# A relational graph layer on one core: weights loaded first, means read from the statistics tile, six of eight normalisations on GpSimd, every fourth mask on ScalarE, filler matmuls in the first PE gaps

## The chip, the cores and the metric

One core of a Trainium2 chip runs the whole kernel. The metric is the device time of one execution in microseconds (us), lower is better. PE is TensorE, DVE VectorE, ACT ScalarE, POOL GpSimd; SP is SyncE, which here only issues DMAs.

## The reference, cut to what matters

There are 128 graphs (B) of 128 nodes (N) with 128 features (D), all fp32, and an int32 adjacency per graph whose entries are 0 or 1. The reference knows 40 relations, but entries above 1 never occur in these inputs, so that only relation 1, the "loop" direction, gives something:

```
h   = relu((x - mean(x)) / sqrt(var(x) + 1e-5))       # per node
p   = h @ W_loop.T
g   = p @ Wg_loop.T
v   = (p + b_loop) * sigmoid(g + bg_loop)
agg = (adj == 1).T @ v                                # per graph
out = x + relu(agg)
```

A general path for the other relations stands behind a branch at the end of the kernel. It is taken only if a sum over the adjacency says that an entry is neither 0 nor 1, and isn't taken here.

## The kernel before, in words

The graphs are worked on in 32 groups of 4 (GROUP), and two groups make a chunk (CHUNK), which is what one load or store of 512 KB moves. All of x and adj has its own place in SBUF (x_all, adj_all), the output is written over x_all and stored from there. Each engine has a queue written out by hand, with semaphores between the queues; nothing is scheduled by a planner. For group g these steps are done:

- row_stats(g) on DVE (L500): two bn_stats, each on two graphs, give per node a count, a mean and a sum of squared deviations for each graph, into the tile stats.
- coefficients, once per chunk, on POOL (L304 to L312): var_eps, mean_neg (the mean times -1), rstd as var_eps to the power -0.5, and shift = mean_neg * rstd. coef_ready is given behind the last.
- normalise(g), one instruction per graph into xn: POOL (L324) and DVE (L519) compute (x + mean_neg) * rstd, ACT (L393) computes x * rstd + shift. shares(g) says who takes which of the four graphs: in an even group POOL 3 and DVE 1; in an odd group POOL 2, DVE 1, ACT 1; in the first two groups DVE 2 and ACT 2.
- turn_rows(g) on PE (L715): four transposes into PSUM. It waits for all engines that normalised.
- relu_turned(g) on ACT (L404) writes hT_hi, rounded to fp32r; low_part(g) on DVE (L545) writes the remainder hT_lo.
- seed(g) on ACT (L411) writes both biases into the PSUM tile that the products add to.
- products(g) on PE: per graph hi by w_hi (L728), hi by w_lo (L729), lo by w_hi (L733), 256 columns wide: p and g at once.
- sigmoid(g) on ACT (L426), messages(g) on DVE (L535).
- edges(g) on POOL (L335) converts the group's adjacency to fp32 into one of four mask slots (MASKS). watch(c) on ACT (L432) sums the adjacency of chunk c for the branch at the end.
- aggregate(g) on PE (L750), output(g) on DVE (L560), and a store on SP (L228).

The loops run over t. PE does turn_rows(t+2), products(t+1), aggregate(t). DVE does messages(t), normalise(t+3), output(t-1), low_part(t+2), row_stats(t+6). ACT does normalise(t+3), relu_turned(t+2), seed(t+2), sigmoid(t+1) and in even t watch. POOL does, in even t, the coefficients of the chunk that holds group t+4, then edges(t+1), then normalise(t+4). xn has four slots, so normalise(g) waits until group g-4 is turned.

Before the loop: ACT's queue issues the two bias rows and then the two 64 KB weight matrices (L375 to L378), SP's queue the loads of x and adj. PE runs four matmuls on zeros, spreads the biases over the partitions with one matmul (L699), turns the weights (L688, L689), multiplies them (L691), and turns group 0. ACT copies bias_all out of PSUM, seeds group 0, and only then copies the turned weights (L443, L444, L446). At the end SP issues three stores: groups 30, the first half of 31, and the second half.

Of the kernel before, what the change touches and what calls it, by code (L numbers as in the profile page):

```python
# [12 lines left out]
GROUP = 4  # L13
# [5 lines left out]
def build(nc, x, adj, W_fwd, W_bwd, W_loop, Wg_fwd, Wg_bwd, Wg_loop,  # L19
# [12 lines left out]
    XN = 4  # L32

    ctx = ExitStack()
    with ctx:
# [16 lines left out]
        stats = sb("stats", [128, 2, PAIRS, 6])  # L52
        mean_neg = sb("mean_neg", [128, 2, CG])
        var_eps = sb("var_eps", [128, 2, CG])
        rstd = sb("rstd", [128, 2, CG])
        shift = sb("shift", [128, 2, CG])
# [44 lines left out]
        first_pow = sem("first_pow")  # L101
# [3 lines left out]
        pow_ready = sem("pow_ready")  # L105
# [3 lines left out]
        normed_act = sem("normed_act")  # L109
# [6 lines left out]
        mask_ready = sem("mask_ready")  # L116
        summed = sem("summed")
# [81 lines left out]
        def shares(g):  # L199

            if g < 2:
                return range(0), range(0, 2), range(2, 4)
            if g % 2 == 0:
                return range(0, 3), range(3, 4), range(4, 4)
            return range(0, 2), range(2, 3), range(3, 4)

        def act_norms(g):

            return g + 1 if g < 2 else 2 + (g - 1) // 2
# [11 lines left out]
        def _(sp):  # L221
# [16 lines left out]
            load_tile(x_all, x, 0, 0, GROUP, x_first)  # L238
            load_tile(x_all, x, GROUP, GC, CG - GROUP, x_loaded[0])
# [18 lines left out]
            sp.wait_ge(half_out, 1)  # L258
            store_tile((GROUPS - 1) * GROUP, (GROUPS - 1) * GC, GROUP // 2)
# [33 lines left out]
        def _(pool):  # L293
# [7 lines left out]
            def coefficients(p, lo, hi, var_done, pow_done, at, done):  # L301

                st = stats[:, p, lo // 2:hi // 2, :].rearrange("p k (e f) -> p k e f", e=2)
                pool.tensor_scalar(var_eps[:, p, lo:hi].rearrange("p (k e) -> p k e", e=2), st[:, :, :, 2],  # L304
                                   1.0 / D, EPS, ALU.mult, ALU.add).then_inc(var_done, 1)
                pool.tensor_scalar(mean_neg[:, p, lo:hi].rearrange("p (k e) -> p k e", e=2), st[:, :, :, 1],
                                   -1.0, 0.0, ALU.mult, ALU.add)
                pool.wait_ge(var_done, at)
                pool.tensor_tensor(rstd[:, p, lo:hi], var_eps[:, p, lo:hi], minus_half[:, lo:hi], ALU.pow  # L309
                                   ).then_inc(pow_done, 1)  # L310
                pool.wait_ge(pow_done, at)
                pool.tensor_tensor(shift[:, p, lo:hi], mean_neg[:, p, lo:hi], rstd[:, p, lo:hi], ALU.mult  # L312
                                   ).then_inc(done, 1)

            def normalise(g):

                s, p = g % XN, g // CHUNK % 2
                if g % CHUNK == 0:
# [3 lines left out]
                for j in shares(g)[0]:  # L322
# [15 lines left out]
            def chunk_coefficients(c):  # L338

                pool.wait_ge(stats_ready, c + 1)  # L340
                if c >= 2:
                    pool.wait_ge(normed_dve, (c - 1) * CHUNK)
                    pool.wait_ge(normed_act, act_norms((c - 1) * CHUNK - 1))
                coefficients(c % 2, GROUP if c == 0 else 0, CG, var_ready, pow_ready, c + 1, coef_ready)

            pool.wait_ge(first_stats, 1)
            coefficients(0, 0, GROUP, first_var, first_pow, 1, first_coef)
            chunk_coefficients(0)
            chunk_coefficients(1)
# [23 lines left out]
        def _(act):  # L373
            act.preload_act_table(ACT.Sigmoid)  # L374
            act.dma_start(bias_row[0:1, 0, :], b_loop).then_inc(bias_loaded, 16)  # L375
            act.dma_start(bias_row[0:1, 1, :], bg_loop).then_inc(bias_loaded, 16)
# [3 lines left out]
            def normalise(g):  # L380

                s, p = g % XN, g // CHUNK % 2
                if not shares(g)[2]:
                    return
                if g == 0:
                    act.wait_ge(first_coef, 1)
                else:
                    act.wait_ge(coef_ready, g // CHUNK + 1)
                if g >= XN:
                    act.wait_ge(turned, g - XN + 1)  # L390
# [437 lines left out]
```

## Time and profile before

| | us |
|---|---|
| median of 3 runs | 113.37 (111.84 to 114.14) |
| profiled execution, its own time | 112.11 |
| its span in the profile | 110.3 |
| busy PE, DVE, ACT, POOL | 98.8, 94.0, 91.8, 87.1 |
| granted TensorE clock in every slice | 9 or more tenths |

The span runs from the first to the last instruction. In the rows further down "xn<-x_all" reads: writes xn, reads x_all; "x3" is a count; L numbers are lines of the kernel before. Instructions of one engine overlap a little, so the next often starts 0.05 to 0.1 us before the recorded end of the one ahead. What an instruction costs its queue is therefore the distance from its start to the next start.

### The profile page before, as it was taken

To read this page: it belongs to the slowest core of one execution; us is meant where nothing else is said; L and a number is where in the kernel's file an instruction comes from. 1 tells how busy PE (TensorE), PEld (TensorE's weight loads), DVE (VectorE), ACT (ScalarE), POOL (GpSimd) and SP (SyncE) were. 2 spreads that over 40 slices of the span, in tenths; PEclk is the share of its full clock that TensorE was granted. 3 is DMA by queue.
4 is the path that set the end of the run, shared out by engine and by line. 5 is a ranking of instruction groups with operands and counts; after the bars stand their busy time and mean duration, and the time that the engine had idled before them with its cause. 6 is when DMAs were issued, how large, how long until landed. Compare 5 with 4: busy or idle time off the path is not lost.

```text
span 110.3 us, 2526 instructions
## 1 busy us (share of the span) xinstructions
PE 98.8 (90%) x780; PEld 92.1 (83%) x780; DVE 94.0 (85%) x202; ACT 91.8 (83%) x153; POOL 87.1 (79%) x182
## 2 busy tenths in 40 slices
PE   5524789899999999999999999999999999999970
PEld 1113569789999999999999999999999999999960
DVE  1508529899999999999999999999999999897780
ACT  4137533999999999999999999999999999999650
POOL 2380790999999999999999999999999999995000
PEclk9999999999999999999999999999999999999999
DMA  2999999999999999999999999980606050515067
GB/s 73 281 311 281 286 290 291 292 291 292 291 317 311 343 332 321 320 320 321 305 320 301 260 309 274 317 222 6 190 6 190 6 180 10 158 38 176 14 185 207
DMA packets 50275, 25.48 MB, mean 231 GB/s; under 512 B 850, under 2 KB 50260, under 8 KB 50260
## 3 DMA queue, kind: packets, MB, share of 16 engines
q1 hardware_dynamic: 49968, 25.17, 81.6%
q10 hardware_dynamic: 292, 0.13, 0.5%
q8 instruction: 7, 0.11, 0.4%
q14 instruction: 8, 0.07, 0.2%
HBM read 16.91 MB, written 8.39 MB: 229 GB/s over the span
## 4 chain that ended last, share of the span: by engine, by line
PE 80%; DMA 5%; POOL 3%; DVE 3%; issue 2%; ACT 2%; ACTq 1%; DVEq 0%; POOLq 0%
PE psum L750 23%; PE psum L715 16%; PE psum L728 14%; PE psum L729 13%; PE psum L733 13%; DMA w_raw<-in_L_gnn_Wg_loop 5%; POOL rstd L309 1%; DVE x_all L560 1%; DVE stats L500 1%; POOL xn L324 1%; PE psum L691 1%; ACT xn L393 1%; ACT hT_hi L404 1%; ACT L374 1%; PE psum L688 0%
## 5 line engine op out<-in xcount | busy, mean ns | idle before, releaser
L728 PE MATMUL psum<-w_hi,hT_hi 128*128 128x256 f32 x128 | 35.1, 307 | 1.8 <-issue 0.8
L750 PE MATMUL psum<-vals,mask 128*128 128x128 f32 x256 | 33.6, 275 | 0.0
L411 ACT ACTIVATE psum<-bias_all 128x1024 f32<-128x1024 f32 x32 | 32.9, 1027 | 0.1
L324 POOL TENSOR_SCALAR xn<-x_all,mean_neg,rstd 128x128 f32<-128x128 f32 x75 | 32.8, 449 | 0.1
L729 PE MATMUL psum<-w_lo,hT_hi 128*128 128x256 f32 x128 | 32.4, 285 | 0.0
L750 PEld LDWEIGHTS psum<-vals,mask 128*128 128x128 f32 x256 | 31.2, 191 | 0.1
L728 PEld LDWEIGHTS psum<-w_hi,hT_hi 128*128 128x128 f32 x128 | 24.7, 193 | 2.8 <-issue 1.7
L309 POOL TENSOR_TENSOR rstd<-var_eps,minus_half 128x8 f32<-128x8 f32 (+1 forms) x17 | 26.6, 1564 | 0.0
L500 DVE BATCH_NORM_STATS2 stats<-x_all 128x6 f32<-128x256 f32 x64 | 23.9, 416 | 2.7 <-DMA x_all<-in_x 2.7
L535 DVE TENSOR_TENSOR vals<-psum,gate 128x512 f32<-128x512 f32 (+1 forms) x33 | 21.7, 659 | 4.3 <-ACT gate L426 4.2
L729 PEld LDWEIGHTS psum<-w_lo,hT_hi 128*128 128x128 f32 x128 | 24.8, 193 | 0.0
L404 ACT ACTIVATE hT_hi<-psum 128x512 fp32r<-128x512 f32 x32 | 19.0, 593 | 5.1 <-PE psum L715 5.1
L545 DVE SCALAR_TENSOR_TENSOR hT_lo<-psum,hT_hi 128x512 fp32r<-128x512 f32 x32 | 21.7, 678 | 1.8 <-ACT hT_hi L404 1.8
L715 PE MATMUL psum<-ident,xn 128*128 128x128 f32 x128 | 20.9, 288 | 1.4 <-ACT xn L393 1.2
L560 DVE SCALAR_TENSOR_TENSOR x_all<-psum,x_all 128x512 f32<-128x512 f32 (+1 forms) x33 | 21.7, 663 | 0.1
L426 ACT ACTIVATE gate<-psum 128x512 f32<-128x512 f32 (+1 forms) x33 | 19.0, 575 | 3.3 <-PE psum L733 3.3
L733 PE MATMUL psum<-w_hi,hT_lo 128*128 128x256 f32 x128 | 20.9, 284 | 0.0
L335 POOL CAST mask<-adj_all 128x512 f32<-128x512 int32 x32 | 19.4, 611 | 0.0
L715 PEld LDWEIGHTS psum<-ident,xn 128*128 128x128 f32 x128 | 14.9, 145 | 4.3 <-POOL xn L324 2.8
L432 ACT ACTIVATE junk<-adj_all,minus_half 128x1024 bf16<-128x1024 int32 x16 | 18.2, 1140 | 0.0
L733 PEld LDWEIGHTS psum<-w_hi,hT_lo 128*128 128x128 f32 x128 | 17.9, 193 | 0.0
L519 DVE TENSOR_SCALAR xn<-x_all,mean_neg,rstd 128x128 f32<-128x128 f32 x34 | 14.8, 439 | 0.3 <-POOL shift L312 0.3
(34 smaller groups left out, 34.2 us busy)
## 6 DMA issues: line engine op xcount, KB each, us to landing
adj_all<-in_adj SPq DMA_DIRECT2D x16, 512.0 KB, 6.6
x_all<-in_x SPq DMA_DIRECT2D x15, 512.0 KB, 6.7
out<-x_all SPq DMA_DIRECT2D x15, 512.0 KB, 4.4
x_all<-in_x SPq DMA_DIRECT2D x2, 256.0 KB, 3.1
out<-x_all SPq DMA_DIRECT2D x1, 256.0 KB, 2.5
out<-x_all SPq DMA_DIRECT2D x2, 128.0 KB, 2.5
w_raw<-in_L_gnn_W_loop ACTq DMA_DIRECT2D x1, 64.0 KB, 3.2
w_raw<-in_L_gnn_Wg_loop ACTq DMA_DIRECT2D x1, 64.0 KB, 5.3
```

What stands on the lines that cost most here:

```text
L309: pool.tensor_tensor(rstd[:, p, lo:hi], var_eps[:, p, lo:hi], minus_half[:, lo:hi], ALU.pow).then_inc(pow_done, 1)
L324: last = pool.tensor_scalar(xn[:, s, j * D:j * D + D], x_all[:, g * GC + j * D:g * GC + j * D + D], mean_neg[:, p, k:k + 1], rstd[:, p, k: ...
L411: nc.scalar.activation(prod_ps[s].rearrange("p g a d -> p g (a d)"), bias_all[:, :, :].rearrange("p a d -> p (a d)").unsqueeze(1) .to_broa ...
L500: last = nc.vector.bn_stats(stats[:, c % 2, (g % CHUNK * GROUP + j) // 2, :], x_all[:, g * GC + j * D:g * GC + (j + 2) * D].rearrange("p ( ...
L535: nc.vector.tensor_tensor(per_graph(vals[:, s, :])[:, some, :], prod_ps[s][:, some, 0, :], per_graph(gate[:, s, :])[:, some, :], ALU.mult) ...
L545: nc.vector.scalar_tensor_tensor(out=hT_lo[:, s, :], in0=hT_ps[s], scalar=0.0, in1=hT_hi[:, s, :].bitcast(FP32), op0=ALU.max, op1=ALU.subt ...
L560: nc.vector.scalar_tensor_tensor(out=cols, in0=sums_ps, scalar=0.0, in1=cols, op0=ALU.max, op1=ALU.add).then_inc(half_out if more else out ...
L715: last = nc.tensor.transpose(hT_ps[s][:, j * N:j * N + N], xn[:, g % XN, j * D:j * D + D], ident[:, :])
L728: nc.tensor.matmul(to, hi, w_hi[:, :], start=False, stop=False, skip_group_check=True)
L729: nc.tensor.matmul(to, hi, w_lo[:, :], start=False, stop=False, skip_group_check=True)
L733: last = nc.tensor.matmul(to, lo, w_hi[:, :], start=False, stop=True, skip_group_check=True)
L750: last = nc.tensor.matmul(to[:, j * D:j * D + D], mask[:, g % MASKS, j * N:j * N + N], vals[:, s, j * D:j * D + D], start=True, stop=True)
```

## The change

- The weights' DMAs become the first of ACT's queue; the bias rows' DMAs move to SP's queue, behind the first load of x.
- mean_neg, shift and the semaphores for them are gone. normalise reads the mean from the stats tile and subtracts it. stats gets four slots (STAT_SLOTS) instead of two.
- POOL normalises 3 graphs of every group (1 in each of the first two), DVE the rest, ACT none.
- The mask of every group with g % 4 == 3 is made by ACT with a Copy; POOL skips it.
- ACT copies the turned weights out ahead of its first seed. DVE normalises group 0 ahead of the weights' remainders.
- PE gets 15 matmuls on zeros, bf16, 256 columns, whose results nobody reads: 3, 3, 5 and 4, at four places before the loop.
- The first half of the last group is stored from ACT's queue, not SP's.

```diff
@@ SP @@
             load_tile(x_all, x, 0, 0, GROUP, x_first)
+            sp.dma_start(bias_row[0:1, 0, :], b_loop).then_inc(bias_loaded, 16)
+            sp.dma_start(bias_row[0:1, 1, :], bg_loop).then_inc(bias_loaded, 16)
             load_tile(x_all, x, GROUP, GC, CG - GROUP, x_loaded[0])
...
-            sp.wait_ge(half_out, 1)
-            store_tile((GROUPS - 1) * GROUP, (GROUPS - 1) * GC, GROUP // 2)
             sp.wait_ge(out_ready, GROUPS)
             store_tile(B - GROUP // 2, (B - GROUP // 2) * D, GROUP // 2)
@@ shares @@
+        def pool_share(g):
+            return 1 if g < 2 else 3
+        def mask_by_act(g):
+            return g % MASKS == MASKS - 1
+        def masks_before(g, by_act):
+            return sum(mask_by_act(k) == by_act for k in range(g))
+        def mean_of(g, j):
+            k = g % CHUNK * GROUP + j
+            return stats[:, g // CHUNK % STAT_SLOTS, k // 2, 1 + k % 2 * 3:2 + k % 2 * 3]
@@ POOL @@
-                pool.tensor_scalar(mean_neg[:, p, lo:hi].rearrange("p (k e) -> p k e", e=2), st[:, :, :, 1],
-                                   -1.0, 0.0, ALU.mult, ALU.add)
                 pool.wait_ge(var_done, at)
                 pool.tensor_tensor(rstd[:, p, lo:hi], var_eps[:, p, lo:hi], minus_half[:, lo:hi], ALU.pow
-                                   ).then_inc(pow_done, 1)
-                pool.wait_ge(pow_done, at)
-                pool.tensor_tensor(shift[:, p, lo:hi], mean_neg[:, p, lo:hi], rstd[:, p, lo:hi], ALU.mult
                                    ).then_inc(done, 1)
...
-                        mean_neg[:, p, k:k + 1], rstd[:, p, k:k + 1], ALU.add, ALU.mult)
+                        mean_of(g, j), rstd[:, p, k:k + 1], ALU.subtract, ALU.mult)
...
+            normalise(0)
             chunk_coefficients(0)
+            normalise(1)
             chunk_coefficients(1)
...
-                if live(t + 1):
+                if live(t + 1) and not mask_by_act(t + 1):
                     edges(t + 1)
@@ ACT @@
-            act.dma_start(bias_row[0:1, 0, :], b_loop).then_inc(bias_loaded, 16)
-            act.dma_start(bias_row[0:1, 1, :], bg_loop).then_inc(bias_loaded, 16)
...
+            def edges(g):
+                act.wait_ge(adj_loaded[g // CHUNK], 16)
+                if g >= MASKS:
+                    act.wait_ge(summed, g - (MASKS - 1))
+                nc.scalar.activation(mask[:, g % MASKS, :], adj_all[:, g * GC:g * GC + GC], ACT.Copy
+                                     ).then_inc(mask_act, 1)
...
             for t in range(GROUPS):
-                if live(t + 3):
-                    normalise(t + 3)
...
                 if t % CHUNK == 0:
                     watch(t // CHUNK)
+                if live(t + 2) and mask_by_act(t + 2):
+                    edges(t + 2)
+            act.wait_ge(half_out, 1)
+            act.dma_start(
+                out[B - GROUP:B - GROUP // 2, :, :].rearrange("b n d -> n b d"),
+                x_all[:, (B - GROUP) * D:(B - GROUP // 2) * D].rearrange("p (b d) -> p b d", b=GROUP // 2)
+            ).then_inc(stored, 16)
@@ DVE @@
-                if g % CHUNK == 0 and c >= 2:
-                    dve.wait_ge(coef_ready, c - 1)
+                if g % CHUNK == 0 and c >= STAT_SLOTS:
+                    dve.wait_ge(normed_pool, (c - STAT_SLOTS + 1) * CHUNK)
...
-                for j in shares(g)[1]:
+                for j in range(pool_share(g), GROUP):
...
+            normalise(0)
             split_weights(0)
-            normalise(0)
             split_weights(1)
@@ PE @@
+            def keep_busy(times, where):
+                for _ in range(times):
+                    nc.tensor.matmul(bank[where][:, 0:256], zeros[:, 0:128], zeros[:, 0:256], start=True, stop=True)
+            keep_busy(3, 1)
             pe.wait_ge(ones_ready, 1)
             pe.wait_ge(bias_loaded, 32)
...
             turn_weights(w_raw[:, 0, :], w_raw[:, 1, :], w_gT[:, :], w_turned, w_gT_ready, 1)
+            keep_busy(3, 1)
...
             turn_rows(0)
+            keep_busy(5, 1)
             pe.wait_ge(w_lo_ready, 2)
             products(0)
             turn_rows(1)
+            keep_busy(4, 6)
             products(1)
```

How the queues change, at three places. POOL's queue over the chunk that holds groups 4 and 5 and the next one's first rows, before (rstd is the power, xn a normalisation, mask an adjacency conversion):

```order
L304 TENSOR_SCALAR var_eps<-stats 128x8
L306 TENSOR_SCALAR mean_neg<-stats 128x8
L309 TENSOR_TENSOR rstd<-var_eps,minus_half 128x8
L312 TENSOR_TENSOR shift<-mean_neg,rstd 128x8
L335 CAST mask<-adj_all 128x512
L324 TENSOR_SCALAR xn<-x_all,mean_neg,rstd 128x128 x3
L335 CAST mask<-adj_all 128x512
L324 TENSOR_SCALAR xn<-x_all,mean_neg,rstd 128x128 x2
L304 TENSOR_SCALAR var_eps<-stats 128x8
```

POOL's queue over groups 4 to 7 now:

```order
L305 TENSOR_SCALAR var_eps<-stats 128x8
L308 TENSOR_TENSOR rstd<-var_eps,minus_half 128x8
L333 CAST mask<-adj_all 128x512
L322 TENSOR_SCALAR xn<-x_all,stats,rstd 128x128 x3
L333 CAST mask<-adj_all 128x512
L322 TENSOR_SCALAR xn<-x_all,stats,rstd 128x128 x3
L305 TENSOR_SCALAR var_eps<-stats 128x8
L308 TENSOR_TENSOR rstd<-var_eps,minus_half 128x8
L322 TENSOR_SCALAR xn<-x_all,stats,rstd 128x128 x3
L333 CAST mask<-adj_all 128x512
L322 TENSOR_SCALAR xn<-x_all,stats,rstd 128x128 x3
```

Two short instructions per chunk are gone, one normalisation per chunk has come, and in every second chunk the first of the two conversions is gone.

ACT's queue from its start to its first sigmoid, before:

```order
L375 DMA bias_row<-in_L_gnn_b_loop 1x128
L376 DMA bias_row<-in_L_gnn_bg_loop 1x128
L377 DMA w_raw<-in_L_gnn_W_loop 128x128
L378 DMA w_raw<-in_L_gnn_Wg_loop 128x128
L437 ACTIVATE bias_all<-psum 128x256
L411 ACTIVATE psum<-bias_all 128x1024
L443 ACTIVATE w_gT<-psum 128x128
L444 ACTIVATE w_hi<-psum 128x128
L446 ACTIVATE w_hi<-psum 128x128
L393 ACTIVATE xn<-x_all,shift,rstd 128x128 x2
L411 ACTIVATE psum<-bias_all 128x1024
L404 ACTIVATE hT_hi<-psum 128x512
```

The same stretch now:

```order
L374 DMA w_raw<-in_L_gnn_W_loop 128x128
L375 DMA w_raw<-in_L_gnn_Wg_loop 128x128
L424 ACTIVATE bias_all<-psum 128x256
L427 ACTIVATE w_gT<-psum 128x128
L428 ACTIVATE w_hi<-psum 128x128
L398 ACTIVATE psum<-bias_all 128x1024
L433 ACTIVATE w_hi<-psum 128x128
L398 ACTIVATE psum<-bias_all 128x1024
L391 ACTIVATE hT_hi<-psum 128x512
```

The weights come ahead of everything, the first seed (L398) stands behind the two weight copies, and no normalisation is left in the queue.

PE's queue from the weights to the first products of group 0, now (before, the same without the rows that read only zeros):

```order
L691 MATMUL psum<-zeros 128x256 x3
L696 MATMUL psum<-bias_row,ones 128x256
L678 MATMUL psum<-ident,w_raw 128x128
L679 MATMUL psum<-ident,w_raw 128x128
L681 MATMUL psum<-w_gT,w_raw 128x128
L691 MATMUL psum<-zeros 128x256 x3
L710 MATMUL psum<-ident,xn 128x128 x4
L691 MATMUL psum<-zeros 128x256 x5
L723 MATMUL psum<-w_hi,hT_hi 128x256
```

## Rows read from the trace of the kernel before

**Rows 1.** The chain that ended last: start us, us, what; the start.

```profile
1.97 5.34 DMA w_raw<-in_L_gnn_Wg_loop
7.45 0.45 PE psum L688
...
9.58 0.77 ACT xn L393 x2
...
13.13 0.21 PE psum L728
...
23.46 0.66 PE psum L715 x4
```

**Rows 2.** Who waited for whom: us in total, times, longest us.

```profile
PEld psum L715 <- POOL xn L324: 2.8, 14, 0.3
```

**Rows 3.** POOL in order of time, one turn of its loop: start us, us.

```profile
59.18 0.20 POOL L304 TENSOR_SCALAR var_eps<-stats 128x8 f32<-128x8 f32 x1
59.46 0.20 POOL L306 TENSOR_SCALAR mean_neg<-stats 128x8 f32<-128x8 f32 x1
59.62 1.64 POOL L309 TENSOR_TENSOR rstd<-var_eps,minus_half 128x8 f32<-128x8 f32 x1
61.34 0.20 POOL L312 TENSOR_TENSOR shift<-mean_neg,rstd 128x8 f32<-128x8 f32 x1
61.48 0.61 POOL L335 CAST mask<-adj_all 128x512 f32<-128x512 int32 x1
62.08 1.31 POOL L324 TENSOR_SCALAR xn<-x_all,mean_neg,rstd 128x128 f32<-128x128 f32 x3
...
63.93 0.88 POOL L324 TENSOR_SCALAR xn<-x_all,mean_neg,rstd 128x128 f32<-128x128 f32 x2
64.89 0.20 POOL L304 TENSOR_SCALAR var_eps<-stats 128x8 f32<-128x8 f32 x1
```

**Rows 4.** DVE in order of time, the same stretch.

```profile
61.57 0.60 DVE L519 TENSOR_SCALAR xn<-x_all,mean_neg,rstd 128x128 f32<-128x128 f32 x1
62.09 0.68 DVE L560 SCALAR_TENSOR_TENSOR x_all<-psum,x_all 128x512 f32<-128x512 f32 x1
62.70 0.67 DVE L545 SCALAR_TENSOR_TENSOR hT_lo<-psum,hT_hi 128x512 fp32r<-128x512 f32 x1
63.29 0.75 DVE L500 BATCH_NORM_STATS2 stats<-x_all 128x6 f32<-128x256 f32 x2
63.97 0.67 DVE L535 TENSOR_TENSOR vals<-psum,gate 128x512 f32<-128x512 f32 x1
64.56 0.33 DVE L519 TENSOR_SCALAR xn<-x_all,mean_neg,rstd 128x128 f32<-128x128 f32 x1
64.81 0.68 DVE L560 SCALAR_TENSOR_TENSOR x_all<-psum,x_all 128x512 f32<-128x512 f32 x1
```

**Rows 5.** The last normalisations of POOL and DVE, in order of time.

```profile
98.22 0.92 POOL L324 TENSOR_SCALAR xn<-x_all,mean_neg,rstd 128x128 f32<-128x128 f32 x2
98.48 0.34 DVE L519 TENSOR_SCALAR xn<-x_all,mean_neg,rstd 128x128 f32<-128x128 f32 x1
```

**Rows 6.** ACT's groups of the page: busy us, mean ns, idle before.

```profile
L411 ACT ACTIVATE psum<-bias_all 128x1024 f32<-128x1024 f32 x32 | 32.9, 1027 | 0.1
L404 ACT ACTIVATE hT_hi<-psum 128x512 fp32r<-128x512 f32 x32 | 19.0, 593 | 5.1 <-PE psum L715 5.1
L432 ACT ACTIVATE junk<-adj_all,minus_half 128x1024 bf16<-128x1024 int32 x16 | 18.2, 1140 | 0.0
```

**Rows 7.** A DMA issue of the page: queue, KB, us from issue to landing.

```profile
w_raw<-in_L_gnn_W_loop ACTq DMA_DIRECT2D x1, 64.0 KB, 3.2
```

**Rows 8.** POOL at the start, in order of time.

```profile
6.08 0.20 POOL L312 TENSOR_TENSOR shift<-mean_neg,rstd 128x4 f32<-128x4 f32 x1
```

**Rows 9.** The chain that ended last, of 100 us to the end.

```profile
101.14 0.12 PE psum L728
```

**Rows 10.** SP's queue in order of time, the last stores.

```profile
106.52 1.49 SPq L228 DMA_DIRECT2D out<-x_all  x3
```

More of the change, by code:

```diff
@@ L32, in build @@
     XN = 4
+    STAT_SLOTS = 4
     ctx = ExitStack()
@@ L51, in build @@
         mask = sb("mask", [128, MASKS, GROUP * N])
-        stats = sb("stats", [128, 2, PAIRS, 6])
-        mean_neg = sb("mean_neg", [128, 2, CG])
+        stats = sb("stats", [128, STAT_SLOTS, PAIRS, 6])
         var_eps = sb("var_eps", [128, 2, CG])
         rstd = sb("rstd", [128, 2, CG])
-        shift = sb("shift", [128, 2, CG])
         minus_half = sb("minus_half", [128, CG])
@@ L299, in _, with coefficients @@
             pool.wait_ge(half_ready, 1)
[L301 to L303 removed]
+            def coefficients(c, lo, hi, var_done, at, done):
+                p = c % 2
+                st = stats[:, c % STAT_SLOTS, lo // 2:hi // 2, :].rearrange("p k (e f) -> p k e f", e=2)
                 pool.tensor_scalar(var_eps[:, p, lo:hi].rearrange("p (k e) -> p k e", e=2), st[:, :, :, 2],
                                    1.0 / D, EPS, ALU.mult, ALU.add).then_inc(var_done, 1)
[L306 to L307 removed]
                 pool.wait_ge(var_done, at)
                 pool.tensor_tensor(rstd[:, p, lo:hi], var_eps[:, p, lo:hi], minus_half[:, lo:hi], ALU.pow
[L310 to L312 removed]
                                    ).then_inc(done, 1)
@@ L317, in normalise @@
                 s, p = g % XN, g // CHUNK % 2
-                if g % CHUNK == 0:
+                if g == 0:
+                    pool.wait_ge(first_coef, 1)
+                elif g % CHUNK == 0 or g == 1:
                     pool.wait_ge(coef_ready, g // CHUNK + 1)
@@ L321, in normalise @@
                     pool.wait_ge(turned, g - XN + 1)
-                for j in shares(g)[0]:
+                for j in range(pool_share(g)):
                     k = g % CHUNK * GROUP + j
@@ L374, in _ @@
             act.preload_act_table(ACT.Sigmoid)
-            act.dma_start(bias_row[0:1, 0, :], b_loop).then_inc(bias_loaded, 16)
-            act.dma_start(bias_row[0:1, 1, :], bg_loop).then_inc(bias_loaded, 16)
             act.dma_start(w_raw[:, 0, :], W_loop).then_inc(w_loaded, 16)
             act.dma_start(w_raw[:, 1, :], Wg_loop).then_inc(w_loaded, 16)
[L380 to L390, printed above, removed]
-                for j in shares(g)[2]:
-                    k = g % CHUNK * GROUP + j
-                    last = nc.scalar.activation(
-                        xn[:, s, j * D:j * D + D], x_all[:, g * GC + j * D:g * GC + j * D + D], ACT.Identity,
-                        bias=shift[:, p, k:k + 1], scale=rstd[:, p, k:k + 1])
-                last.then_inc(normed_act, 1)
+            def edges(g):
[4 more added lines that the diff above has]
+                                     ).then_inc(mask_act, 1)
             def relu_turned(g):
@@ L438, in _ @@
                                  ).then_inc(bias_ready, 1)
+            act.wait_ge(w_turned, 1)
+            nc.scalar.activation(w_gT[:, :], bank[6][:, 128:256], ACT.Copy).then_inc(w_gT_ready, 1)
+            nc.scalar.activation(w_hi[:, 0:D], bank[6][:, 0:D], ACT.Copy).then_inc(w_hi_ready, 1)
             act.wait_ge(bits_set, 1)
@@ L520, in normalise @@
                         xn[:, s, j * D:j * D + D], x_all[:, g * GC + j * D:g * GC + j * D + D],
-                        mean_neg[:, c % 2, k:k + 1], rstd[:, c % 2, k:k + 1], ALU.add, ALU.mult)
+                        mean_of(g, j), rstd[:, c % 2, k:k + 1], ALU.subtract, ALU.mult)
                 last.then_inc(normed_dve, 1)
```

31 lines of the change are left out of this document (6 added, 25 removed).

## The prediction, made before the changed kernel ran

> **What bounds the kernel now.** I read the chain that ended last first. It is PE almost from end to end, but it starts with a DMA: the second weight matrix is issued at 1.97, flies for 5.34, and PE turns the weights only from 7.45. The first transposes of group 4, from which on the loop runs evenly, start at 23.46 [rows 1]. So there are two things: a start of 23.5 us and a loop. For the loop I read who waits for whom. PE's weight loads for the transposes wait for a POOL normalisation 14 times, 2.8 us in total, 0.2 each and 0.3 at most [rows 2]: once per two groups, from group 4 to group 30. I then read POOL in order of time. From one var_eps to the next, 59.18 to 64.89, it has no gap: POOL works 5.71 us per two groups and sets the period [rows 3]. Without its wait PE would need 5.71 - 0.20 = 5.51. DVE, the same way, by the distance from one start to the next: an output 0.61, a low part 0.59, a statistics pair 0.68, vals 0.59, and a normalisation 0.25 at 64.56 but 0.52 at 61.57 [rows 4]. With both normalisations short that is 2 x (0.61 + 0.59 + 0.68 + 0.59 + 0.25) = 5.44; the 0.27 more makes 5.71. The long one ends (62.17) just behind POOL's mask conversion (62.09), so I read it as DVE held up by POOL. Three engines stand within 0.3 us of each other per two groups: POOL 5.71, PE 5.51, DVE 5.44 plus what POOL takes from it.
>
> **The loop, part by part.** POOL loses mean_neg (59.46 to 59.62, 0.16 us) and shift (61.34 to 61.48, 0.14, and some 0.08 of waiting for the power's semaphore ahead of it). It gains one normalisation: from 62.08 to 63.93 stand three of them and a conversion, which takes 0.60 (61.48 to 62.08), so one costs (63.93 - 62.08 - 0.60) / 3 = 0.42. It loses a conversion of 0.60 in every second chunk, 0.30 on average [rows 3]. The sum is 5.71 - 0.16 - 0.22 + 0.42 - 0.30 = 5.45; some of the 0.28 between var_eps and mean_neg stays as the wait ahead of the power. POOL falls under PE's 5.51, but only by 0.06. The order helps: the coefficients of a chunk can start as soon as DVE's statistics pair ends, where POOL was 0.8 us late before (59.18 against the end of a pair, 5.71 before 63.29 + 0.75, or 58.33). So POOL has that as a reserve, and PE's wait should go. That gives 2.8 - 0.33 (the first of the 14 belongs to the start) = 2.5 us. Bounds: 0, if another engine holds the period at 5.71, and 2.5. I take 2.5, because both other engines' own work lies under 5.51 in the rows.
>
> DVE normalises one graph per group as before and reads the mean from another tile, which costs nothing: the operand has the same shape. What can change is the hold-up. The mean of the two (0 and 0.27) is already 0.13 per normalisation. POOL now spends 6 x 0.42 of 5.5 us in normalisations and 0.9 in conversions. Does a POOL normalisation hold up DVE? The one place that shows it is at the end: two of POOL's run from 98.22 and take 0.92 instead of 0.88, and DVE's own, from 98.48 on in the middle of them, takes 0.34, hardly more than at 64.56 [rows 4, 5]. So DVE got through and POOL paid 0.04. If the hold-up of 0.27 falls away DVE runs at 5.44, if one remains at 5.71. By my own placing of the new order, DVE's even normalisation comes 3.24 us after a statistics pair ended (61.57 against 58.33), the power ends 2.0 after it, and so it falls in POOL's first row of normalisations in a chunk, or at its very end, not in the middle of a conversion. I take no hold-up.
>
> The Trainium skill speaks against that: its page "SBUF — State Buffer", section "Who interferes with whom", says that a fast-mode tensor_scalar of DVE and any GpSimd instruction take a shared pair of ports as an exclusive lock, so that the one that comes second is blocked until the first has finished. The conversion at 61.48 fits it, the DVE normalisation at 98.48 does not. What it would do here is the first and the last of the rivals.
>
> ACT loses a 128x128 normalisation per two groups (the two of the start cost 0.77 together in the chain, 0.39 each [rows 1]) and gets a 128x512 conversion per four groups. The trace has no conversion on ACT. The nearest rows are 128x512 from PSUM, 0.59, and 128x1024 from SBUF, 1.14 [rows 6]; I take 0.6, which is 0.3 per two groups. ACT gets 0.1 lighter. It sits in odd iterations, those without watch, so no sigmoid comes later. Were it 1.14, ACT would be 0.2 heavier than before per two groups and would still have had waits of 5.1 us in its transposed rows. DVE's waits for the statistics slots and PE's waits for other semaphores ask for things long done.
>
> **The start.** Call W the moment when PE starts to turn the weights, 7.45 now. Their DMAs go out 1.2 us (first) and about 0.7 us (second) earlier, ahead of the bias rows. Bounds: with the flight of 5.34 unchanged W is 6.75. With the flight of the other matrix, 3.2 [rows 7], the weights land near 4.5, but then the bias product stands ahead in PE's queue: the bias rows now go out behind the first load of x on SP, land near 4, and their product with its copies takes PE until about 5.4. So W lies between 5.4 and 6.75. I take 5.65, since the second matrix moves up to where the first one was issued, and that one flew 3.2.
>
> From W to the transposes of group 4 it is 23.46 - 7.45 = 16.0 us now. Anew, relative to W: weights turned, copied and multiplied, 1.85 (the chain needs 7.45 to 9.58, 2.13, with one small copy behind it [rows 1]). Three fillers, 256 columns each, at the spacing of 0.21 that a 256-column matmul has at 13.13: 2.5. Transposes of group 0, 1.0: 3.5. They need no wait: the first coefficients were done at 6.28 before [rows 8] and come earlier now, while ACT's normalisation used to stand behind the weight copies, at 9.58. Five fillers, 1.07: 4.6. ACT meanwhile has two copies, seed 1.03, a copy, seed 1.03, relu 0.59 [rows 6], done by 4.1 to 4.3. Products of group 0 at W + 4.6. They had a spacing of 0.21 (the 1.2 GHz level; the granted share is full all along) and in the loop have 0.12 [rows 1, 9], the 2.4 GHz level. Before, PE stood still again and again on this way (the chain goes to ACT at 9.58), and its first products were still slow. Now it works without a break from W + 1.0, for 3.6 us ahead of them. So I take 0.12 for the products of group 0: 12 matmuls, 1.4, done at W + 6.1. If the fast level comes only behind them, it costs 1.1.
>
> Then transposes of group 1 to W + 6.5. ACT's sigmoid and relu, 0.59 each [rows 6], allow the products of group 1 at 7.5, done at 8.9. DVE: vals and low part of these groups and one normalisation until 8.5, then the statistics of groups 4 and 5, four at 0.36: 9.9. POOL: coefficients in 1.9, conversion 0.6, three normalisations 1.3: 13.8. Transposes of group 4 at W + 13.85, POOL last as before. This saves 16.0 - 13.85 = 2.15, and W itself 7.45 - 5.65 = 1.8. Start: -4.0. Bounds: W at 6.75 and the slow level give -1.8; W at 5.4 gives -4.2. Fillers ahead of the weights cost nothing (PE waits for a DMA there); those behind group 0 cost 0.4 at most and are in the sum.
>
> **The end.** SP issues its last three stores from 106.52 over 1.49 [rows 10], about 0.5 each, the last at about 107.5, while the last output ends at 107.15. With one on ACT the last can go at about 107.2: -0.3, between -0.5 and 0 (if two queues issue no faster than one).
>
> **The sum.** -4.0 - 2.5 - 0.3 = -6.8. On the profiled execution's own time of 112.11 (span 110.3 and 1.8 around it) that is 105.3. This execution lies 1.26 under the median of the runs, 113.37, so on the median's scale 106.6.
>
> **Rivals.** (1) DVE takes over as the bound of the loop: each two groups hold one hold-up of 0.27, the period stays at 5.71 and the 2.5 us are not gained. For it: DVE's 5.44 is only 0.07 under PE, so any hold-up over 0.07 counts. Against it: the DVE row of rows 5. Time: 106.6 + 2.5 = 109.1. A hold-up of 0.1 to 0.2 lies between the two.
> (2) The start gives little: the weights land hardly earlier, since they fly amid the loads of x either way, and the matmuls keep the slow level. Start -1.8 instead of -4.0: 108.8. For it: of two equal matrices issued 0.4 apart one flew 3.2 and the other 5.34, so the flight depends on something the rows don't show.
> (3) Slower: POOL's normalisations hold DVE up for their whole length, as the page named above has it for the second comer. Two DVE normalisations per two groups, each waiting up to 0.42, make 5.44 + 0.84 = 6.28, which is 0.57 more than 5.71, over 14 turns +8.0. With the start and end at -4.3 the time is 113.4 + 3.7 = 117.1. It decides from a hold-up of about 0.29 per normalisation on: then the period is 6.02, and 14 x 0.31 eats the 4.3. Against it: 98.48, and that DVE would drift to a place where it waits less.
>
> **How the numbers follow.** The forecast as it stands gets 0.60, rival 1 and what lies between 0.24, rival 2 0.12, rival 3 0.04. Each of the first three is more than 2% (2.3 us, about what a measurement of this kernel can tell) under 113.37, that is under 111.1. Only both losses together (106.6 + 2.5 + 2.2 = 111.3) would end within 2%. Faster 0.91, same 0.06, slower 0.03. The range goes from 104.2 (every term at its better bound, 0.2 and 0.2, and two us of scatter between runs, 111.84 to 114.14) to 110.0, which takes in either loss alone.
>
> **What would show it.** Right: PE's wait for POOL's normalisations in the loop gone and 0.2 or less in total per four groups; a period of 11.0 to 11.1 us over four groups; the first turned weights before 6.8; products of group 0 at a spacing of 0.12 and transposes of group 4 near 19.5. Wrong: DVE normalisations of 0.6 on a regular beat with the period at 5.7, which is rival 1; or transposes of group 4 later than 21.5, which is rival 2. A POOL that still ends its normalisations just ahead of PE's transposes would mean that I mis-sized POOL's 5.45.

## The result, and the profile after

The changed kernel takes 134.26 us (median of 4 runs, 134.0 to 134.74) against 113.75 us for the kernel before (median of 4, 111.84 to 114.39; one run more than in the table above): a ratio of 1.193, with a 95% interval of 1.178 to 1.208. The ratio takes, of the kernel before, only the runs within 1.5% of its fastest; the two medians alone give 1.180. It is 19% slower, where I had forecast 6% faster and given "slower" a chance of 0.03. The span went from 110.3 to 132.2 us. Line numbers below are those of each kernel's own file.

The page of the changed kernel, busy time by engine, the groups that changed most (busy us, mean ns, idle time before them and what ended most of it), and the chain that ended last:

```profile
PE 105.3 (80%) x795; PEld 95.4 (72%) x795; DVE 97.9 (74%) x204; ACT 88.2 (67%) x142; POOL 116.6 (88%) x157
...
POOL 75%; issue 8%; PE 8%; DVE 2%; DMA 2%; ACT 1%; SPq 1%; POOLq 0%
...
L322 POOL TENSOR_SCALAR xn<-x_all,stats,rstd 128x128 f32<-128x128 f32 x92 | 72.7, 799 | 1.0
L391 ACT ACTIVATE hT_hi<-psum 128x512 fp32r<-128x512 f32 x32 | 19.1, 597 | 31.3 <-PE psum L710 31.3
...
L509 DVE TENSOR_SCALAR xn<-x_all,stats,rstd 128x128 f32<-128x128 f32 x36 | 15.8, 450 | 17.0 <-POOL rstd L308 17.0
```

The first of the groups carries the loss. A normalisation on POOL takes 0.80 us; three of them took 1.31 together before [rows 3], 0.44 each. There are 92 of them, and 92 x 0.36 is 33 us of new work on the engine that set the period already. PE and DVE wait for POOL now, and ACT for PE's transposes behind it. The waits, in the form of [rows 2]:

```profile
PEld psum L710 <- POOL xn L322: 21.0, 16, 1.7
```

POOL in order of time, over the same stretch as [rows 3]:

```profile
62.18 0.19 POOL L305 TENSOR_SCALAR var_eps<-stats 128x8 f32<-128x8 f32 x1
62.46 1.66 POOL L308 TENSOR_TENSOR rstd<-var_eps,minus_half 128x8 f32<-128x8 f32 x1
64.07 0.61 POOL L333 CAST mask<-adj_all 128x512 f32<-128x512 int32 x1
64.67 2.35 POOL L322 TENSOR_SCALAR xn<-x_all,stats,rstd 128x128 f32<-128x128 f32 x3
66.97 0.61 POOL L333 CAST mask<-adj_all 128x512 f32<-128x512 int32 x1
67.57 2.35 POOL L322 TENSOR_SCALAR xn<-x_all,stats,rstd 128x128 f32<-128x128 f32 x3
69.89 0.20 POOL L305 TENSOR_SCALAR var_eps<-stats 128x8 f32<-128x8 f32 x1
```

All other rows are as they were: the power 1.66 against 1.64, the conversion 0.61. Only three normalisations take 2.35. The turn is 7.71 us (62.18 to 69.89) against 5.71, both with two conversions. Two things were changed in that instruction: the operation (subtract for add) and the place of its first scalar (the statistics tile for a packed one). DVE's normalisation had the same two edits, and its quick ones still take 0.33 to 0.35 us in this trace (its mean is 450 ns, where it was 439).

### The profile page after: what moved, and what is told of

Read it like the earlier page. It is cut to its first block, busy times and chain, and to the rows that moved or that the text cites. A ratio compares the mean times of both kernels' runs of the same rounds, so it can differ in the third digit from the quotient of the medians.

```text
span 132.2 us, 2498 instructions
## 1 busy us (share of the span) xinstructions
PE 105.3 (80%) x795; PEld 95.4 (72%) x795; DVE 97.9 (74%) x204; ACT 88.2 (67%) x142; POOL 116.6 (88%) x157
## 4 chain that ended last, share of the span: by engine, by line
POOL 75%; issue 8%; PE 8%; DVE 2%; DMA 2%; ACT 1%; SPq 1%; POOLq 0%
POOL xn L322 48%; POOL rstd L308 19%; POOL mask L333 6%; DMA bias_row<-in_L_gnn_bg_loop 2%; PE psum L745 2%; POOL var_eps L305 2%; PE psum L723 1%; PE psum L724 1%; PE psum L728 1%; DVE x_all L550 1%; DVE stats L490 1%; PE psum L710 1%; PE psum L696 1%; ACT psum L398 1%; SPq L223 0%
## 5 line engine op out<-in xcount | busy, mean ns | idle before, releaser
L322 POOL TENSOR_SCALAR xn<-x_all,stats,rstd 128x128 f32<-128x128 f32 x92 | 72.7, 799 | 1.0
L745 PE MATMUL psum<-vals,mask 128*128 128x128 f32 x256 | 34.7, 280 | 2.9 <-POOL mask L333 2.9
L723 PE MATMUL psum<-w_hi,hT_hi 128*128 128x256 f32 x128 | 35.7, 310 | 0.3 <-ACT hT_hi L391 0.3
L398 ACT ACTIVATE psum<-bias_all 128x1024 f32<-128x1024 f32 x32 | 33.0, 1030 | 0.0
L710 PEld LDWEIGHTS psum<-ident,xn 128*128 128x128 f32 x128 | 14.0, 143 | 22.7 <-POOL xn L322 21.0
L509 DVE TENSOR_SCALAR xn<-x_all,stats,rstd 128x128 f32<-128x128 f32 x36 | 15.8, 450 | 17.0 <-POOL rstd L308 17.0
L724 PEld LDWEIGHTS psum<-w_lo,hT_hi 128*128 128x128 f32 x128 | 25.3, 198 | 0.0
L333 POOL CAST mask<-adj_all 128x512 f32<-128x512 int32 x24 | 14.6, 609 | 0.0
```

The costliest lines, as they stand in the source:

```text
L322: last = pool.tensor_scalar(xn[:, s, j * D:j * D + D], x_all[:, g * GC + j * D:g * GC + j * D + D], mean_of(g, j), rstd[:, p, k:k + 1], AL ...
L333: pool.tensor_copy(mask[:, g % MASKS, :], adj_all[:, g * GC:g * GC + GC]).then_inc(mask_ready, 1)
L398: nc.scalar.activation(prod_ps[s].rearrange("p g a d -> p g (a d)"), bias_all[:, :, :].rearrange("p a d -> p (a d)").unsqueeze(1) .to_broa ...
L710: last = nc.tensor.transpose(hT_ps[s][:, j * N:j * N + N], xn[:, g % XN, j * D:j * D + D], ident[:, :])
L723: nc.tensor.matmul(to, hi, w_hi[:, :], start=False, stop=False, skip_group_check=True)
L724: nc.tensor.matmul(to, hi, w_lo[:, :], start=False, stop=False, skip_group_check=True)
```

## The experiments

First I separated the operation from the operand.

**e1: both undone on POOL.** The negated mean is computed into its tile again, POOL adds it, and everything else of the change stays.

```diff
+                pool.tensor_scalar(mean_neg[:, p, lo:hi].rearrange("p (k e) -> p k e", e=2), st[:, :, :, 1],
+                                   -1.0, 0.0, ALU.mult, ALU.add)
...
-                        mean_of(g, j), rstd[:, p, k:k + 1], ALU.subtract, ALU.mult)
+                        mean_neg[:, p, k:k + 1], rstd[:, p, k:k + 1], ALU.add, ALU.mult)
```

> The changed kernel, with the negated mean computed into its own tile again and POOL normalising with (add, mult) from it; DVE still subtracts from the statistics tile; all other edits stay (no shift, no ACT normalisations, ACT masks, weights first, fillers, store on ACT). Both theories (the operation, the operand's place) expect POOL's normalisation back at 0.44 us (0.80 in the changed kernel) and so a time near what my sum had: period of about 11.1 us per four groups, 105 to 109 us. If the slow normalisation has some third cause (load of POOL, neighbours), it stays at 0.8 and the time at 134 us.

**e2: the operand undone, the operation kept.** The difference to e1:

```diff
-                                   -1.0, 0.0, ALU.mult, ALU.add)
+                                   1.0, 0.0, ALU.mult, ALU.add)
...
-                        mean_neg[:, p, k:k + 1], rstd[:, p, k:k + 1], ALU.add, ALU.mult)
+                        mean_neg[:, p, k:k + 1], rstd[:, p, k:k + 1], ALU.subtract, ALU.mult)
```

> As e1, but the mean is stored with its own sign in the packed tile and POOL uses (subtract, mult). Theory 'operation' (subtract is slow on POOL): 0.80 us per normalisation and 134 to 137 us. Theory 'operand' (the scalar out of the statistics tile is slow): 0.44 us and the time of e1.

**e3: the operation undone, the operand kept.** It is the changed kernel with one word different. POOL's graphs get x + mean, so it doesn't compute the layer.

```diff
-                        mean_of(g, j), rstd[:, p, k:k + 1], ALU.subtract, ALU.mult)
+                        mean_of(g, j), rstd[:, p, k:k + 1], ALU.add, ALU.mult)
```

> The changed kernel with one word changed on POOL: add for subtract, the scalar still out of the statistics tile; POOL's graphs get x + mean in place of x - mean. Theory 'operation': 0.44 us and the time of e1 or 0.2 less. Theory 'operand': 0.80 us and 134 us.

POOL's normalisations in e1, e2 and e3 (one row of each trace, busy us and mean ns):

```profile
L325 POOL TENSOR_SCALAR xn<-x_all,mean_neg,rstd 128x128 f32<-128x128 f32 x92 | 41.4, 464 | 1.1
```

```profile
L325 POOL TENSOR_SCALAR xn<-x_all,mean_neg,rstd 128x128 f32<-128x128 f32 x92 | 72.7, 798 | 1.1
```

```profile
L322 POOL TENSOR_SCALAR xn<-x_all,stats,rstd 128x128 f32<-128x128 f32 x92 | 40.3, 450 | 1.0
```

e1 and e2 read the same tile and differ only in the operation and a sign: 464 and 798 ns, and 108.09 us (median of 4) against 138.38 us (one run). e3 reads the statistics tile and adds: 450 ns and 106.25 us (one run), 28 us less than the changed kernel. So the operand's place costs nothing, and subtract costs 0.35 us per instruction. e1 is faster than the kernel before: a ratio of 0.959, interval 0.953 to 0.965.

**e4: eight forms beside each other.** From group 4 on POOL takes form g % 8; to, x_j, mean_j and rstd_j are the operands that the instruction had before. Most forms leave out or change the normalisation, so it doesn't compute the layer; its one run took 116.99 us.

```diff
+                    if form == 0:
+                        last = pool.tensor_scalar(to, x_j, mean_j, rstd_j, ALU.subtract, ALU.mult)
+                    elif form == 1:
+                        last = pool.tensor_scalar(to, x_j, mean_j, rstd_j, ALU.add, ALU.mult)
+                    elif form == 2:
+                        last = pool.tensor_scalar(to, x_j, rstd_j, mean_j, ALU.mult, ALU.add)
+                    elif form == 3:
+                        last = pool.tensor_scalar(to, x_j, rstd_j, mean_j, ALU.mult, ALU.subtract)
+                    elif form == 4:
+                        last = pool.tensor_scalar(to, x_j, mean_j, None, ALU.subtract)
+                    elif form == 5:
+                        last = pool.tensor_scalar(to, x_j, mean_j, None, ALU.add)
+                    elif form == 6:
+                        last = pool.tensor_scalar(to, x_j, 0.5, 1.5, ALU.subtract, ALU.mult)
+                    else:
+                        last = pool.tensor_scalar(to, x_j, 0.5, 1.5, ALU.add, ALU.mult)
```

> The changed kernel, POOL's normalisations of group g in the form g % 8 from group 4 on, each on a line of its own: (subtract, mult), (add, mult), (mult, add), (mult, subtract), subtract alone, add alone, and the first two with constants. These leave out or change the normalisation. Theory 'operation': every form with subtract takes 0.75 to 0.80, every form without 0.44 or less. Theory 'operand': all of the first six 0.80, the two with constants 0.2 to 0.44.

The groups of POOL, in the order in which the trace has them; L327, L329, ... L341 are forms 0 to 7:

```profile
L327 POOL TENSOR_SCALAR xn<-x_all,stats,rstd 128x128 f32<-128x128 f32 x17 | 13.3, 791 | 0.3
L339 POOL TENSOR_SCALAR xn<-x_all 128x128 f32<-128x128 f32 x12 | 7.5, 649 | 0.4
L333 POOL TENSOR_SCALAR xn<-x_all,rstd,stats 128x128 f32<-128x128 f32 x9 | 7.3, 815 | 0.0
L337 POOL TENSOR_SCALAR xn<-x_all,stats 128x128 f32<-128x128 f32 x12 | 7.2, 614 | 0.0
L335 POOL TENSOR_SCALAR xn<-x_all,stats 128x128 f32<-128x128 f32 x12 | 7.1, 604 | 0.0
L331 POOL TENSOR_SCALAR xn<-x_all,rstd,stats 128x128 f32<-128x128 f32 x9 | 4.2, 470 | 0.3
L329 POOL TENSOR_SCALAR xn<-x_all,stats,rstd 128x128 f32<-128x128 f32 x9 | 3.9, 447 | 0.0
L341 POOL TENSOR_SCALAR xn<-x_all 128x128 f32<-128x128 f32 x12 | 3.3, 298 | 0.0
```

With two scalars from tiles: (add, mult) 447, (mult, add) 470, (subtract, mult) 791, (mult, subtract) 815. With constants, (add, mult) takes 298 and (subtract, mult) 649. Subtract beside mult costs 0.35 each time. But my expectation missed on the single operations: subtract alone takes 604 and add alone 614, alike, and both more than add and mult together. So "subtract is slow" is not quite the rule. What the eight rows fit is that a pair made of add and mult is quick and every other form here is not. I didn't try other pairs, and why the engine prices the forms so stays open.

**e5: the operation alone, in the kernel before.** It shows whether the harm needs the rest of the change. POOL's normalisation and DVE's both go from add to subtract. ACT's graphs get the wrong sign of the shift, so it doesn't compute the layer either.

```diff
-                                   -1.0, 0.0, ALU.mult, ALU.add)
+                                   1.0, 0.0, ALU.mult, ALU.add)
...
-                        mean_neg[:, p, k:k + 1], rstd[:, p, k:k + 1], ALU.add, ALU.mult)
+                        mean_neg[:, p, k:k + 1], rstd[:, p, k:k + 1], ALU.subtract, ALU.mult)
...
-                        mean_neg[:, c % 2, k:k + 1], rstd[:, c % 2, k:k + 1], ALU.add, ALU.mult)
+                        mean_neg[:, c % 2, k:k + 1], rstd[:, c % 2, k:k + 1], ALU.subtract, ALU.mult)
```

> The kernel before with one thing changed: the mean is stored with its own sign and POOL and DVE use (subtract, mult) for (add, mult). ACT's graphs get the wrong sign of the shift. If the operation on POOL is the whole cause, it does the harm without any other part of the change: 5 normalisations of 0.79 instead of 0.44 make POOL's turn 5.71 + 5 x 0.35 = 7.46 us per two groups, 14 turns give +24 us, so about 137 us. If the harm needs six normalisations or another part of the change, it stays under 125 us.

It took 137.31 us (one run), as worked out, beside 113.62 for the kernel before on the same chip (median of 7, 111.28 to 114.4); the row of its trace:

```profile
L324 POOL TENSOR_SCALAR xn<-x_all,mean_neg,rstd 128x128 f32<-128x128 f32 x75 | 59.4, 799 | 0.1
```

Subtract for add in the kernel before makes it 24 us slower; DVE's share of the edit can't be the cause, since DVE subtracts in e1, e3 and e6 too and they are quick. The 24 us are more than the whole change loses (20.5 us), so the rest of the change must gain. The rest of the experiments size these gains, all on a kernel without subtract on POOL.

**e6 and e7: the negated mean off POOL.** e3 has the queue that I priced but doesn't compute the layer. e6 gives POOL the same queue and does: ACT negates the means, from the third chunk on. In e7 DVE does it.

```diff
+            def negate(c):
+                act.wait_ge(stats_ready, c + 1)
+                act.wait_ge(normed_pool, (c - 1) * CHUNK)
+                nc.scalar.activation(mean_neg[:, c % 2, :].rearrange("p (k e) -> p k e", e=2),
+                                     stats[:, c % STAT_SLOTS, :, :].rearrange("p k (e f) -> p k e f", e=2)[:, :, :, 1],
+                                     ACT.Copy, scale=-1.0).then_inc(mean_ready, 1)
...
+                if t % CHUNK == 0 and live(t + 4):
+                    negate((t + 4) // CHUNK)
```

> e1 with mean_neg made by ACT from the third chunk on (one 128x8 Copy with scale -1 between seed and sigmoid of even iterations), so that POOL has the queue that I priced. Theory 'my sum was right but for the operation': POOL under PE, period near 11.0 us per four groups, 106 us, 2 us under e1. If ACT's extra 0.2 us delays the sigmoids or POOL waits for ACT, it stays at e1's 108 or comes above.

> As e6 with mean_neg on DVE behind vals in even iterations. DVE's own 5.44 us per two groups becomes about 5.52 to 5.56, at or just over PE's 5.51: 106 to 107 us. If POOL's held locks cost DVE 0.27 once per two groups as in e1, the period is 5.8 and the time 109 us.

e6 took 106.18 us (median of 4, 105.7 to 106.36), e7 106.71 (106.33 to 107.08), on e5's chip, where the fastest run of the kernel before took 111.28. e6 is the fastest of the kernels that compute the layer, and faster than both kernels of this study; e11 below, which differs from it in the queue of one store, has a ratio of 0.945 (0.936 to 0.954) to the kernel before. The page of e6: the chain by engine, and two groups.

```profile
PE 88%; DMA 3%; ACT 2%; DVE 2%; issue 1%; SPq 1%; ACTq 0%
...
L329 POOL TENSOR_SCALAR xn<-x_all,mean_neg,rstd 128x128 f32<-128x128 f32 x92 | 41.3, 462 | 1.1
...
L727 PEld LDWEIGHTS psum<-ident,xn 128*128 128x128 f32 x128 | 15.4, 144 | 0.2 <-POOL xn L329 0.2
```

The chain is PE's again, and PE's wait for POOL is 0.2 us in total where it was 2.8 [rows 2]. PE's transposes in e6 stand 11.06 us apart over four groups:

```profile
61.21 0.60 PE L727 MATMUL psum<-ident,xn 128*128 128x128 f32 x4
...
72.27 0.60 PE L727 MATMUL psum<-ident,xn 128*128 128x128 f32 x4
```

In e1, where POOL still negates the means, POOL has 61% of the chain and PE only 20%. Its two turns are unequal, 5.89 us with two conversions (61.88 to 67.77) and, from the power of one turn to that of the next, 5.59 with one (56.73 to 62.32):

```profile
56.73 1.64 POOL L311 TENSOR_TENSOR rstd<-var_eps,minus_half 128x8 f32<-128x8 f32 x1
...
61.88 0.20 POOL L306 TENSOR_SCALAR var_eps<-stats 128x8 f32<-128x8 f32 x1
62.16 0.20 POOL L308 TENSOR_SCALAR mean_neg<-stats 128x8 f32<-128x8 f32 x1
62.32 1.64 POOL L311 TENSOR_TENSOR rstd<-var_eps,minus_half 128x8 f32<-128x8 f32 x1
...
67.77 0.20 POOL L306 TENSOR_SCALAR var_eps<-stats 128x8 f32<-128x8 f32 x1
```

The mean of the two is 5.74, no better than the 5.71 of before. So e1's 4% don't come from the loop: its transposes of group 4 stand at 19.95, where they stood at 23.46 [rows 1]. The loop's gain hangs on those 0.16 us of POOL per turn. e3, on e1's chip, has e1's queues without them and takes 106.25, and PE has 85% of its chain.

**e8: e1 without the fillers.**

```diff
-            keep_busy(3, 1)
...
-            keep_busy(3, 1)
...
-            keep_busy(5, 1)
...
-            keep_busy(4, 6)
```

> e1 without the 15 filler matmuls. The fillers' own time behind group 0 is 1.07 us at the slow spacing. Theory 'fillers bring the fast level earlier': without them the products of group 0 run at 0.21 spacing, their part of the start is 1 us longer or the same, time 108 to 109 us. Theory 'fillers only cost': 0.5 us under e1.

109.25 us (109.11 to 109.5) against e1's 108.09. The two ran on different chips, and on e8's the kernel before scatters from 111.28 to 114.4, so I don't rest on the 1.16 us. I read the two chains. e1 first, with fillers (L694), then e8:

```profile
8.93 1.07 PE psum L694 x5
10.00 0.28 PE psum L726
...
10.45 0.12 PE psum L726
...
11.77 0.65 PE psum L713 x4
```

```profile
10.16 0.55 PE psum L724
10.71 0.21 PE psum L725
...
13.06 0.87 PE psum L711 x4
```

The products of group 0 start together, at 10.0 and 10.16. With fillers they reach the spacing of 0.12 (the 2.4 GHz level) at 10.45, without them they stay at 0.21 (the 1.2 GHz level) to their end, and the transposes of group 1 come at 11.77 against 13.06. In this pair the fillers are worth 1.3 us there, and 1.1 at the transposes of group 4 (19.95 against 21.01). But the moment varies by run: the chain of e7, also with fillers, keeps 0.21 for all products of group 0 with both weight parts, and its transposes of group 1 come at 12.67, 0.4 ahead of e8's. There is one trace without fillers, so 0.4 to 1.3 us is what these traces can say.

**e9, e10, e11, e12: one part of e6 undone or moved at a time**, on one chip. The edits to e6, in the order e9, e10, e11, e12:

```diff
-            sp.dma_start(bias_row[0:1, 0, :], b_loop).then_inc(bias_loaded, 16)
-            sp.dma_start(bias_row[0:1, 1, :], bg_loop).then_inc(bias_loaded, 16)
...
+            act.dma_start(bias_row[0:1, 0, :], b_loop).then_inc(bias_loaded, 16)
+            act.dma_start(bias_row[0:1, 1, :], bg_loop).then_inc(bias_loaded, 16)
             act.dma_start(w_raw[:, 0, :], W_loop).then_inc(w_loaded, 16)
```

```diff
-            return g % MASKS == MASKS - 1
+            return False
```

```diff
+            sp.wait_ge(half_out, 1)
+            store_tile((GROUPS - 1) * GROUP, (GROUPS - 1) * GC, GROUP // 2)
...
-            act.wait_ge(half_out, 1)
-            act.dma_start(
...
```

```diff
-            sp.dma_start(bias_row[0:1, 0, :], b_loop).then_inc(bias_loaded, 16)
-            sp.dma_start(bias_row[0:1, 1, :], bg_loop).then_inc(bias_loaded, 16)
...
             act.dma_start(w_raw[:, 1, :], Wg_loop).then_inc(w_loaded, 16)
+            act.dma_start(bias_row[0:1, 0, :], b_loop).then_inc(bias_loaded, 16)
+            act.dma_start(bias_row[0:1, 1, :], bg_loop).then_inc(bias_loaded, 16)
```

> e6 with the DMA order of the kernel before: both bias rows and then the weights on ACT's queue, none on SP's. My sum gave the earlier weights 1.8 us. In e6's chain the bias rows (landing at 4.5) and not the weights decide when PE turns the weights (5.79). If the weights land near 7.4 as before, the time is 1.4 to 1.8 us over e6's 106.2. If the rest of the start (x, ACT's seeds) sets the pace anyway, it is within 0.5 us.

> e6 with every mask made by POOL again. Adds 0.60 us per four groups to POOL, 10.72 + 0.6 = 11.3 against PE's 11.0: 0.3 us in each of 7 turns of four groups, 2 us over e6, 108 us, with PE waiting for POOL's normalisations again. If POOL still had more reserve than I priced, the same as e6.

> e6 with the first half of the last group stored from SP's queue as before. My sum priced the move at 0.3 us: 106.5. If the two queues share what issues, no difference.

> e6 with the bias rows on ACT's queue behind the weights, so that SP's second load of x goes out 0.7 us earlier (its landing, 6.5, holds DVE's second statistics). If that load or the bias rows' landing on SP's queue is what the start waits for, 0.3 to 0.7 us under e6; if the bias rows land later on ACT's queue than on SP's (they have PE's queue behind them), as much above it.

| run | undone or moved | us (4 runs) | ratio to before |
|---|---|---|---|
| e9 | weights behind the bias rows | 108.35 (107.7 to 108.68) | 0.962 (0.952 to 0.972) |
| e10 | masks all on POOL | 106.78 (106.45 to 107.72) | 0.951 (0.940 to 0.961) |
| e11 | last stores all on SP | 106.37 (106.19 to 106.74) | 0.945 (0.936 to 0.954) |
| e12 | bias rows behind the weights | 108.29 (107.8 to 108.93) | 0.960 (0.950 to 0.969) |

e11 is the nearest to e6 on that chip (e6 had 106.18 on another), so I compare with it. The starts of the chains of e9, e12 and e6, in this order:

```profile
2.00 5.66 DMA w_raw<-in_L_gnn_Wg_loop
...
7.79 0.45 PE psum L695
```

```profile
2.42 4.03 DMA bias_row<-in_L_gnn_bg_loop
6.58 1.19 PE psum L713 x2
7.77 0.41 PE psum L695
```

```profile
1.69 2.78 DMA bias_row<-in_L_gnn_bg_loop
4.60 1.19 PE psum L713 x2
5.79 0.41 PE psum L695
```

In all three PE turns the weights (L695) as soon as the later of weights and bias product is there, and the time follows it: 2 us later in e9 and in e12, and 2.0 and 1.9 us more than e11. The second matrix flies 5.66 us when it is issued fourth on ACT's queue, at 2.00 (e9), 3.8 when it is issued second and the bias rows follow (e12), and 3.0 when it is issued second and nothing follows (e6); the bias rows fly 4.03 behind both matrices (e12) and 2.78 on SP's queue. So the earlier weights are worth what I priced, but only because the bias rows went to the other queue.

e10 missed its expectation: 0.4 us over e11, not 2, inside the scatter of the runs. Its POOL turn with two conversions is 5.58 us:

```profile
60.44 0.20 POOL L307 TENSOR_SCALAR var_eps<-stats 128x8 f32<-128x8 f32 x1
...
66.02 0.20 POOL L307 TENSOR_SCALAR var_eps<-stats 128x8 f32<-128x8 f32 x1
```

My price for that was 5.45 + 0.30 = 5.75. The turn stands only 0.05 over e6's 5.53, and 14 of these are 0.7. e11 shows no difference that can be told (0.19 us, and the spans are 104.4 and 104.5).

## Why the prediction was wrong

**The step that failed** is in the loop, part by part: POOL "gains one normalisation: from 62.08 to 63.93 stand three of them and a conversion, ... so one costs 0.42". I counted the instructions and priced all six at what (x + mean_neg) * rstd takes, although the diff turns add into subtract in the same line. The trace of before has no subtract on POOL at all. For ACT's conversion, which had no row either, I gave bounds; for this I gave none. The measured size is 0.79 to 0.80 (e2, e4), 0.35 more for each of 92 instructions. Over a turn of two groups it is 6 x 0.35 = 2.1 us. On e10's 5.58, a turn with two conversions and no subtract, that makes 7.7, and the changed kernel's turn with two conversions is 7.71. Undoing that one word takes the changed kernel from 134.26 to 106.25 us (e3), and e5 shows that the harm needs nothing else of the change.

None of my rivals had this. The one on the slower side, DVE held up by POOL, needed 0.29 per normalisation. What I listed as a sign of an error, "a POOL that still ends its normalisations just ahead of PE's transposes would mean that I mis-sized POOL's 5.45", is what the profile shows.

**The other steps** can be checked on e6 and e3, which have POOL's queue as I priced it:

- The loop. PE as the bound at 5.51 per two groups: e6 has 5.53, and its wait for POOL is gone. POOL's 5.45 was close but for the wrong reason. Its turns in e6, from power to power:

```profile
54.32 1.75 POOL L313 TENSOR_TENSOR rstd<-var_eps,minus_half 128x8 f32<-128x8 f32 x1
56.17 1.44 POOL L329 TENSOR_SCALAR xn<-x_all,mean_neg,rstd 128x128 f32<-128x128 f32 x3
...
59.72 1.64 POOL L313 TENSOR_TENSOR rstd<-var_eps,minus_half 128x8 f32<-128x8 f32 x1
61.30 0.61 POOL L340 CAST mask<-adj_all 128x512 f32<-128x512 int32 x1
...
65.33 1.75 POOL L313 TENSOR_TENSOR rstd<-var_eps,minus_half 128x8 f32<-128x8 f32 x1
```

  They are 5.40 with one conversion and 5.61 with two, 5.50 on the mean. The sum took a whole conversion, 0.60, out of every second turn; the difference is 0.21. A conversion starts 1.58 after the power (59.72 to 61.30), a normalisation 1.85 after it (54.32 to 56.17), and the three normalisations of the shorter turn take 1.44 for 1.31. With both conversions in every turn e10 has 5.58, so the masks on ACT were hardly needed.
- DVE keeps up. In e6 its normalisations between 55 and 80 us take 0.33 to 0.40, none the 0.60 of [rows 4]. One of them, at 56.96, falls into POOL's three from 56.17 on:

```profile
56.96 0.33 DVE L526 TENSOR_SCALAR xn<-x_all,stats,rstd 128x128 f32<-128x128 f32 x1
```

  DVE isn't delayed, and POOL's three take 1.44 instead of 1.31. That is [rows 5] again: POOL pays here, not DVE. The exclusive lock that the Trainium skill describes on the page "SBUF — State Buffer", section "Who interferes with whom", would hold the second comer for the first one's whole instruction, and the DVE normalisations at 56.96 here and at 98.48 in [rows 5] are not held in that way. A conversion does go with a DVE normalisation of 0.60 (e1, at 64.00, once in four groups, beside a conversion from 63.91 to 64.52).
- The start. I had PE turning the weights at 5.65 and group 4 transposed at 19.5. e6 has 5.79 and 19.43, the changed kernel itself 5.73 for the first. The earlier weights are worth 2.0 us (e9) where I had 1.8. I had the products of group 0 at the quick spacing throughout; in e6 and e3 they reach it on their way.
- The end. -0.3 was priced, and 0 to 0.2 can't be told from nothing (e11).
- The sum. 106.6 was forecast, and e6 with 106.18 and e3 with 106.25 are near it. That e6 meets it so closely is partly luck. On the profiled executions the forecast was 105.3 after 112.11, and e6 has 106.14: the start gave the 4.0, the stretch from the transposes of group 4 to those of group 31 went from 77.1 to 75.0 us (2.1 where I had 2.5), and the end gave nothing. So the sum was 0.8 us off there. The 1.26 that I had added, because the median of before lay that much above its profiled execution, made up for it: e6's median lies on its own. The mechanisms of start and loop were right, except that the kernel that I priced was not the one in the diff.

## What to carry to other kernels

Price an instruction by its operations, both of the pair, as well as by its engine, shape and operands: an edit that saves a 0.16 us helper by changing add to subtract can cost twice that in each instruction that used it. On an engine that sets the period, look in the trace for a row of the very pair of operations, and where there is none, run it by itself first. When engines stand within a few per cent of each other, a saving counts only up to the next one, and a small helper moved to the engine with idle time (here 128x8 on ACT) can carry the whole gain of the loop.

## What the runs showed of the hardware that I had not expected

- GpSimd's tensor_scalar of 128x128 fp32 takes 447 to 470 ns as add and mult in either order, 791 to 815 with subtract for add, and about 610 for add or subtract alone: one operation costs more than the two together. With constants in place of the scalars (add, mult) is 298 and (subtract, mult) 649. DVE's shows no such difference: its median is 340 ns with add (before) and with subtract (e6).
- The two 64 KB weight matrices, issued first on ACT's queue at 0.8 and 1.2, fly 2.9 and 3.0 us; behind the bias rows the second flies 5.3 (before) to 5.7 (e9). The 0.5 KB bias row behind the two matrices flies 4.0, and the second matrix then 3.8 (e12). All fly amid the loads of x.
